# A layer-norm, wave filter, code correction and FFN block: halves of rows and weights as sums and differences, and one PSUM bank for all three branches

## The reference

```
xn  = layernorm(x)                                 # 8192 tokens of 256 numbers, f32
D   = fractal_dimension(xn)                        # one number, from the first 1024 numbers of xn
x1  = real(ifft(fft(xn) * wave_filter(D, 256)))    # the same 256-point filter for every token
lat = x1 @ W_el + b_el                             # 24 latents
c   = golay_correct(sigmoid(lat) > 0.5)            # 24 bits, up to three of them flipped by the syndrome
wave = x1 + c @ W_le + b_le
ffn  = gelu(xn @ w1 + b1, exact) @ w2 + b2         # 256 -> 1024 -> 256
out  = x + wave + ffn
```

## Time and profile before

| | |
|---|---|
| runs | 452.53, 454.07, 454.49 us |
| profiled execution, its span | 451.6 us (the page gives no other time for it) |
| TensorE busy | 444.3 us, 98% |
| VectorE busy | 260.4 us, 58% |
| ScalarE busy | 196.5 us, 44% |
| GpSimd busy | 26.5 us, 6% |
| HBM read and written | 19.4 MB, 43 GB/s over the span |

### The profile page before, as it was taken

The page is one execution under the profiler, slowest core; times in us unless marked ns, Lnnn a source line. Parts: engine busy times, 40 slices in busy tenths (PEclk is TensorE's granted clock), DMA queues, the critical chain, the costliest instruction groups (busy, mean ns, idle before and its releaser), DMA issues.

```text
span 451.6 us, 8842 instructions
## 1 busy us (share of the span) xinstructions
PE 444.3 (98%) x2976; PEld 402.1 (89%) x2976; DVE 260.4 (58%) x752; ACT 196.5 (44%) x332; POOL 26.5 (6%) x42
## 2 busy tenths in 40 slices
PE   6999999999999999999999999999999999999996
PEld 3889998988999899998998999899898999989896
DVE  5888556465554646547465564746547465564544
ACT  4744444344443543444444343544345434443431
POOL 1601001010000101001010010100001010010000
PEclk9999999999999999999999999999999999999999
DMA  7788100000000000000000000000000000000101
GB/s 227 210 263 248 59 25 25 0 23 23 23 23 23 0 23 23 23 23 23 0 23 23 23 23 14 10 23 23 23 23 15 8 23 23 23 23 0 48 25 47
DMA packets 11308, 19.58 MB, mean 43 GB/s; under 512 B 2691, under 2 KB 4893, under 8 KB 11293
## 3 DMA queue, kind: packets, MB, share of 16 engines
q1 hardware_dynamic: 11298, 19.44, 13.0%
HBM read 11.03 MB, written 8.39 MB: 43 GB/s over the span
## 4 chain that ended last, share of the span: by engine, by line
PE 97%; DMA 1%; DVE 0%; ACT 0%; SPq 0%; issue 0%; DVEq 0%
PE p_o L739 41%; PE p_h L719 39%; PE p_c L753 11%; PE p_t L690 3%; PE p_c L772 2%; DMA w_f<-L_ffn_w 1%; PE p_g L763 1%; PE p_c L827 0%; DVE x_sb L544 0%; PE p_c L837 0%; SPq L214 0%; ACT w_hi L360 0%; DVE x_sb L502 0%; ACT xT_hi L374 0%; SPq L224 0%
## 5 line engine op out<-in xcount | busy, mean ns | idle before, releaser
L319 ACT ACTIVATE h<-p_h,b_sb 128x512 f32<-128x512 f32 x128 | 88.1, 688 | 226.3 <-PE p_h L719 226.2
L450 DVE TENSOR_TENSOR h_lo<-h,h_hi 128x512 fp32r<-128x512 f32 x128 | 90.0, 704 | 110.6 <-ACT h_hi L327 108.7
L739 PE MATMUL p_o<-w_hi,h_hi 128*128 128x256 f32 x512 | 149.7, 292 | 0.0
L739 PE MATMUL p_o<-w_lo,h_hi 128*128 128x256 f32 x512 | 144.5, 282 | 0.0
L739 PE MATMUL p_o<-w_hi,h_lo 128*128 128x256 f32 x512 | 144.4, 282 | 0.0
L739 PEld LDWEIGHTS p_o<-w_hi,h_hi 128*128 128x128 f32 x512 | 97.3, 190 | 2.2 <-DVE h_lo L450 0.5
L739 PEld LDWEIGHTS p_o<-w_lo,h_hi 128*128 128x128 f32 x512 | 97.5, 191 | 1.3
L739 PEld LDWEIGHTS p_o<-w_hi,h_lo 128*128 128x128 f32 x512 | 97.4, 190 | 0.0
L719 PE MATMUL p_h<-xT_hi,w_hi 128*128 128x512 f32 (+1 forms) x258 | 82.1, 399 | 0.8 <-ACT xT_hi L374 0.8
L327 ACT CAST h_hi<-h 128x512 fp32r<-128x512 f32 x128 | 79.6, 622 | 5.6
L719 PE MATMUL p_h<-xT_hi,w_lo 128*128 128x512 f32 (+1 forms) x258 | 79.8, 390 | 0.0
(11 more groups left out here) (95 smaller groups left out, 314.2 us busy)
## 6 DMA issues: line engine op xcount, KB each, us to landing
out<-x_sb SPq DMA_DIRECT2D x31, 256.0 KB, 2.0
x_sb<-L_attn_x SPq DMA_DIRECT2D x15, 512.0 KB, 4.0
w_f<-L_ffn_w SPq DMA_DIRECT2D x3, 512.0 KB, 8.2
x_sb<-L_attn_x SPq DMA_DIRECT2D x2, 256.0 KB, 3.1
w_f<-L_ffn_w SPq DMA_DIRECT2D x2, 256.0 KB, 5.8
basis_sb<-basis SPq DMA_DIRECT2D x1, 256.0 KB, 5.0
out<-x_sb SPq DMA_DIRECT2D x2, 128.0 KB, 1.8
con<-consts SPq DMA_DIRECT2D x1, 144.5 KB, 3.4
```

Source lines behind the costliest of these rows:

```text
L319: nc.scalar.activation(h[m % 2][:], p_h[:, m % 2, :], ACT.Gelu, bias=b1_sb[:, m:m + 1]).then_inc(gelu_done, 1)
L450: nc.vector.tensor_tensor(h_lo[m % HR][:], h[m % 2][:], h_hi[m % HR][:].bitcast(F32), ALU.subtract).then_inc(h_lo_done, 1)
L739: last = mm(p_o[:, j, :], hp[r][:, tok], w[:, m, :], start=(m == 0 and n == 0 and j % 2 == 0), stop=(m == MB - 1 and n == 2), skip_group_c ...
```

## The change

C's two block rows turn into two matrices of half the size: with u = x_a + x_b and v = x_a - x_b of the halves of a row, the sum of the result's halves is u(A + B), the difference v(A - B). So everything is kept in sums and differences. All weights that read xn or write the output are turned too (w1 by rows; w2, W_le and b by columns, with factors of one half).

- GpSimd makes sums and differences of x (`turn`, into `rq`); VectorE normalises them to `uv` (eight instructions of 128x128 in place of four of 128x256), which is transposed where `xn` was. `fr_row` is a row of plain xn for D.
- Of the weights, VectorE turns w1's parts 0 and 1, GpSimd w1's part 2 and w2, into scratch that lies in the late part of `x_sb` (`w1_t`, `w2_t`); ScalarE's rounding and VectorE's subtraction read these. GpSimd's two subtractions go to VectorE. SP's loads of the last four chunks wait for the weights.
- A wave is 24 matmuls of 152 columns (128 and 24), of the same chunk as the FFN, into `p_o`, now one bank a tile: columns 0 to 127 sums, 128 to 175 latents, 176 to 303 differences (`both_halves` leaves the latents out). `down` and `le_products` add to the same bank. `p_c` goes; the small products at the start use `p_m`, in the bank of `p_g`.
- A chunk's correction is one block of four tiles. `down`(0) waits for the read of the latents (`lat_read`), since the latents share the bank.
- VectorE adds half of `rq` to `p_o` (`add_sums`, four of 128x256), GpSimd turns back to rows of the output (`unturn`, two of 128x512), SP stores 512 KB a chunk.
- Chunk 1 (`second_chunk`) has the waves of chunks 0 and 1, the last chunk only its own.

```diff
-        p_o = ps("p_o", [P, CT, E], F32)
-        p_c = ps("p_c", [P, 2, BANK], F32)
+        p_o = ps("p_o", [P, CT, BANK], F32)
...
+            def turn(c, par):
+                pool.wait_ge(x_in[par], 8 * (c - par) + 16)
+                xc = x_chunk(c)
+                nc.gpsimd.tensor_tensor(rq[par][:, :, 0, :], xc[:, :, 0:HF], xc[:, :, HF:E], ALU.add).then_inc(turned, 1)
+                nc.gpsimd.tensor_tensor(rq[par][:, :, 1, :], xc[:, :, 0:HF], xc[:, :, HF:E],
+                                        ALU.subtract).then_inc(turned, 1)
...
+            def unturn(c, par):
+                pool.wait_ge(z_done, CT * (c + 1))
+                xc = x_chunk(c)
+                nc.gpsimd.tensor_tensor(xc[:, :, 0:HF], rq[par][:, :, 0, :], rq[par][:, :, 1, :],
+                                        ALU.add).then_inc(unturned, 1)
+                nc.gpsimd.tensor_tensor(xc[:, :, HF:E], rq[par][:, :, 0, :], rq[par][:, :, 1, :],
+                                        ALU.subtract).then_inc(unturned, 1)
+            def chunk(c, par):
+                unturn(c - 1, 1 - par)
+                pool.wait_ge(unturned, 2 * c)
+                turn(c + 1, 1 - par)
+                inverse_root(c + 1 + HEAD, 1 - par)
...
+            def add_sums(par, tiles=range(CT)):
+                for j in tiles:
+                    nc.vector.scalar_tensor_tensor(out=rq[par][:, j, :, :], in0=rq[par][:, j, :, :], scalar=0.5,
+                                                   in1=both_halves(j), op0=ALU.mult, op1=ALU.add).then_inc(z_done, 1)
...
+            def chunk(c, par, hops, last=False):
+                dve.wait_ge(down_done, MB * c)
+                add_sums(1 - par)
+                hidden_lo(c, 0)
+                hidden_lo(c, 1)
+                correct(c, hops)
...
+            def tail():
+                dve.wait_ge(half_down, 1)
+                add_sums(1, range(HALF))
+                dve.wait_ge(down_done, MB * CHUNKS)
+                add_sums(1, range(HALF, CT))
+                dve.wait_ge(z_done, CT * CHUNKS)
+                dve.wait_ge(tail_out, 2)
+                for k, op in ((0, ALU.add), (1, ALU.subtract)):
+                    nc.vector.tensor_tensor(xc[:, HALF:CT, k * HF:(k + 1) * HF], rq[1][:, HALF:CT, 0, :],
+                                            rq[1][:, HALF:CT, 1, :], op).then_inc(tail_out, 1)
...
             def down(c, m, first=False, tiles=range(CT), done=down_done):
                 pe.wait_ge(h_lo_done, MB * c + m + 1)
                 if m == 0 and not first:
-                    pe.wait_ge(ffn_out, PAIRS * c)
+                    pe.wait_ge(lat_read, c + 1)
...
-                        last = mm(p_o[:, j, :], hp[r][:, tok], w[:, m, :], start=(m == 0 and n == 0 and j % 2 == 0),
+                        last = mm(both_halves(j), hp[r][:, tok], w[:, m, :, :], start=(first and m == 0 and n == 0),
...
+            def wave_products(c, par, first=False):
+                pe.wait_ge(c_ready, 1)
+                if not first:
+                    pe.wait_ge(z_done, CT * c)
+                for j in range(CT):
+                    tok = slice(j * P, (j + 1) * P)
                     n = 0
+                    for k, at in enumerate((0, HF)):
                         for xt, cc in ((xT_hi, c_hi), (xT_hi, c_lo), (xT_lo, c_hi)):
+                            last = mm(p_o[:, j, at:at + WC], xt[par][:, k, tok], cc[:, k * WC:(k + 1) * WC],
+                                      start=(n == 0 and not first), stop=False, skip_group_check=True)
...
+            def chunk(c, par, last=False):
                 for m in range(MB):
                     up(c, par, m)
                     if m == 1:
+                        wave_products(c, par)
+                    if m >= 6 and not last:
+                        transpose_block(c + 1, m - 6)
                     if m == 4:
+                        transpose_corrected(c)
+                    if m == 6:
+                        le_products(c)
                     if m >= 2:
                         down(c, m - 2)
...
+            def second_chunk(c, par):
+                up(c, par, 0)
+                up(c, par, 1)
+                wave_products(c - 1, 1 - par, first=True)
+                up(c, par, 2)
+                up(c, par, 3)
+                transpose_corrected(c - 1, first=True)
+                up(c, par, 4)
+                le_products(c - 1)
+                up(c, par, 5)
+                wave_products(c, par)
```

More of the change, by code:

```diff
@@ L118, in build @@
         rstd = [sb(f"rstd{i}", [P, CT], F32) for i in range(2)]
+        mean2 = [sb(f"mean2{i}", [P, CT], F32) for i in range(2)]
         eps = sb("eps", [P, CT], F32)
@@ L518, in chunk @@
-                hidden_lo(c, 6)
+                then(statistics(c + 1, 1 - par))
+                aggregate(1 - par)
+                dve.wait_ge(le_done, 1)
+                add_sums(1 - par)
+                correct(c, then)
+                for m in range(4, 7):
+                    hidden_lo(c, m)
+                normalise(c + 1, 1 - par)
+                hidden_lo(c, 7)
                 transposed_lo(c + 1, 1 - par, 0)
                 transposed_lo(c + 1, 1 - par, 1)
-                hidden_lo(c, 7)
@@ L565, in _ @@
                 aggregate(0, halves[g])
+            x0 = x_chunk(0)
+            for k, op in ((0, ALU.add), (1, ALU.subtract)):
+                last = nc.vector.tensor_tensor(rq[0][:, HALF:CT, k, :], x0[:, HALF:CT, 0:HF], x0[:, HALF:CT, HF:E], op)
+            then(last)
+            dve.wait_ge(turned_head, 2)
             normalise(0, 0, 0)
             normalise(0, 0, 1)
-            w1_part_lo(0)
+            turn_w1(0)
             for g in range(2):
@@ L572, in _ @@
                                         ALU.subtract).then_inc(t_lo, 1)
-            w1_part_lo(1)
+                if g == 0:
+                    turn_w1(1)
+                w1_part_lo(g)
             w2_part_lo(0)
@@ L578, in _ @@
             hidden_lo(0, 1)
+            w1_part_lo(2)
             hidden_lo(0, 2)
@@ L765, in transpose_corrected, with le_products @@
                 last.then_inc(cor_t, 1)
-            def le_products(c, q):
-                pe.wait_ge(cor_sb, PRIMED + PAIRS * c + q + 1)
+            def le_products(c):
+                pe.wait_ge(cor_sb, c + 1)
                 pe.wait_ge(le_ready, 1)
-                for r in range(2):
-                    last = mm(p_c[:, r, 0:E], cor_T[:, r * P:(r + 1) * P], le3[:], start=False, stop=True,
+                for j in range(CT):
+                    last = mm(both_halves(j), cor_T[:, j * P:(j + 1) * P], le3[:, :, :], start=False, stop=False,
@@ new lines, in chunk, with second_chunk @@
+                down(c, MB - 2)
+                if last:
+                    down(c, MB - 1, tiles=range(HALF), done=half_down)
+                    down(c, MB - 1, tiles=range(HALF, CT))
+                else:
+                    down(c, MB - 1)
+            def second_chunk(c, par):
+                up(c, par, 0)
[8 more added lines that the diff above has]
+                wave_products(c, par)
+                for m in range(MB):
+                    if m == 0:
+                        up(c, par, 6)
+                    if m == 3:
+                        up(c, par, 7)
+                    if m == 4:
+                        transpose_corrected(c)
+                    if m == 6:
+                        le_products(c)
+                        transpose_block(c + 1, 0)
+                    if m == 7:
+                        transpose_block(c + 1, 1)
+                    down(c, m)
```

480 lines of the change are left out of this document (242 added, 238 removed).

## The result

The changed kernel takes 461.86 us (median of five runs, 459.99 to 466.94) against 453.09 (452.53 to 454.49): ratio 1.018, 95% interval 1.0144 to 1.0216 (the launch of 466.94 us counts as slow and is not in the ratio). It is slower by 1.8%; 458.4 us, 1.0% slower, was forecast, and the range held it. The profiled execution has a span of 461.74 us where the kernel before had 451.58.

A forecast was written before the change was run, and what follows sets the result against it. The prediction took TensorE, busy for 98% of the span, as the bound: 451.6 - 6.5 - 1.0 + 9.0 + 1.9 + 0.9 = 455.9 us of span, plus 2.5 for 458.4 us, slower by 1.0%, range 449 to 465.

The forecast's parts named there:

- Wave products: All chunks: 384 matmuls narrowed from 280 to 152 columns take 0.112 us instead of 0.129 each, 6.5 us less.
- Columns (0.076): Rival, 7%: narrow wave products go by their columns at 0.076 us; TensorE would gain 20.4, time 455 us.
- two passes: Rival, 6%: narrow f32r wave products fall back to the two passes of plain f32, 501 us.
- The loop's cover: Loop chunks: down(0)'s wait for the latents' read is covered by 0.1 us, taken as nothing; 0.3 late costs 4 us.
- the forecast's 0.41 + 0.07: Each loop chunk: gain from narrower wave products, plus 0.07 from fewer, larger small blocks (1.0 us over 15).
- The start: Before chunk 1: added VectorE and GpSimd work delays the first up of chunk 1, +9.0 us.
- its lock: Start: VectorE and GpSimd instructions exclude each other, so times add up; 9.0 us with it, 1.5 without.
- The rival's 1.5 us without exclusion: Start, rival, 20%: GpSimd's turns lie beside VectorE's work, so the start costs only +1.5, 450.9 us.
- Chunk 1: Chunk 1 with two waves: waits for cor_T (0.4) and add_sums(0) (some 1.5), +1.9 us, from 0 to 3.
- the sum: Whole kernel: the forecast's terms added to the span before, 451.6 us, giving 455.9 us of span.
- The tail: After the last matmul: additions, GpSimd's unturning and a larger store take longer, +0.9 us.
- The 2.5 us that the sum adds from span to launch: Whole kernel: median launch of 454.07 lay 2.5 above the span before; the same added to 455.9 gives 458.4 us.

The follow-up runs named there:

- e5_wide: Changed kernel with each wave product reading and writing 256 columns instead of 152, results wrong: 461.66 us, one run.
- e4_turn: Changed kernel with GpSimd's turn for the next chunk waiting in the loop until this chunk's latents are read: 459.73 us, one run.
- e7_all: Changed kernel with e2_weights, e3_sums and e4_turn; VectorE also makes fr_row from uv and turns chunk 1's x: 454.22 us, 1.0036 of the kernel before.
- e10_fill: e9_best with idle matmuls in TensorE's start waits and h_lo(1) of chunk 0 ahead of chunk 1's statistics and sums: 452.68 us, 0.9995 of the kernel before.
- e2_weights: Changed kernel with fr_row and all weight turning moved from GpSimd to VectorE: 460.20 us, 1.0174 of the kernel before.
- e9_best: e7_all with ScalarE making fr_row and v halves of uv for chunks 0 and 1, tail additions from PSUM: 452.74 us, 0.9999 of the kernel before.
- e3_sums: Changed kernel with chunk 1's add_sums(0) ahead of statistics and aggregation in VectorE's row: 459.30 us, 1.0137 of the kernel before.

## Why the prediction came out as it did

- **Wave products: right.** 0.110 measured, 0.112 taken; e5_wide shows that the columns hardly count. Columns (0.076) and two passes are out; the load as the cause is argued.
- **The loop's cover: failed.** "That is cover by 0.1. I take nothing": `down`(0) does wait, and with it gone a chunk is 0.16 us shorter (e4_turn). Over chunks 2 to 14 that is 1.7 us (350.38 against 348.67 in e4_turn; chunk 14 took 26.81 in both). With it the change brings 27.27 - 26.81 = 0.46 a chunk, about the forecast's 0.41 + 0.07.
- **The start: right in its lock, right in size partly by luck.** +8.7 against +9.0; `h_lo`(0) ends at 20.38 (21.1), `h_lo`(5) at 36.18 (36.4). But `fr_row` was taken at 0.35 an instruction, with one left at 9.1, and costs 1.36 to 1.50, until 12.94; against that, six GpSimd instructions of 128x512 were put ahead of `h_lo`(0), and its chain waited for two (`turn_w2`(0)). The two errors roughly cancel. The rival's 1.5 us without exclusion stays untested: e7_all and e10_fill are free of the lock only by giving GpSimd's work to VectorE, and there 5.2 and 3.9 us remain.
- **Chunk 1: the wait was named, the clock was not.** The forecast had 1.9 us of stalls. The failed step is that a wait costs its own length: in the profiled execution some 7 us at half clock followed and cost 3.1 us, the largest term that the sum lacks. Not every execution pays it: with the same wait, e2_weights kept its clock.
- **The tail: mis-sized.** +1.4 instead of +0.9.

The missing terms, 3.1 + 1.7 + 0.5 - 0.3, are 5.0 us of span, and the profiled span is 461.74 where the sum had 455.9. The other 0.8 us are not taken apart; stalls in chunk 1 beyond 1.9 are in them, since at full clock it takes 32.72, a loop chunk and a second wave 26.81 + 2.64. By the median, which lies lower than this run, the forecast is 3.5 us short. The 2.5 us that the sum adds from span to launch set a median against the span of another launch; within the profiled launch it is 1.8 (463.53 and 461.7).

One description ahead of the prediction is wrong in a detail: a bank of `p_o` has sums in columns 0 to 127, latents in 128 to 151 (both parts add up there) and differences in 152 to 279. No number rests on it.

## What to carry to other kernels

Turning work into fewer columns pays only down to a floor for each pair of weight load and matmul, here 0.11 us; what pays for it must be hidden where the engines have room, and a start is where they have least. Price a wait of TensorE by what its clock may do afterwards as well, and look at more than one execution before you do. Idle matmuls in the waits go with a full clock: in the start, e9_best had some 7 us at half clock and e10_fill none, and their mean granted clocks, over eleven launches each, are 0.989 to 0.994 and 0.997 to 1.000 (it won no time there). GpSimd is no free second VectorE: on two SBUF inputs their times add up.

## What the runs showed of the hardware

VectorE and GpSimd do not always take turns. In the profiled run of e3_sums VectorE asked at 9.62, and two instructions of 0.35 us took 11.97, while GpSimd ran one instruction after another at its own speed. VectorE, then GpSimd, in that run:

```profile
9.62 11.97 DVE L631 TENSOR_TENSOR x_sb<-w_f 128x256 f32<-128x256 f32 x2
```

```profile
7.42 5.16 POOL L356 TENSOR_SCALAR fr_row<-x_sb,mv,rstd 1x256 f32<-1x256 f32 x4
...
12.56 2.47 POOL L327 TENSOR_TENSOR x_sb<-w_f 128x512 f32<-128x512 f32 x2
14.99 2.47 POOL L320 TENSOR_TENSOR x_sb<-w_f 128x512 f32<-128x512 f32 x2
17.43 1.25 POOL L312 TENSOR_TENSOR rq<-x_sb 128x512 f32<-128x512 f32 x1
18.65 1.25 POOL L313 TENSOR_TENSOR rq<-x_sb 128x512 f32<-128x512 f32 x1
```

Chunk 1 started at 50.27 there, 5.8 us later than in the profiled run of the same start code, and that launch took 465.41 where the other four took 458.75 to 459.48. Whether the spread of the changed kernel's launches (459.99 to 466.94) comes from this, from the clock in chunk 1 or from both was not profiled. VectorE's additions with one input in PSUM were not held off: in the tail they ran at 0.37 each beside GpSimd's 0.73.
